# Depthwise convolutions of one layer: joined bands as the stationary operand, wide moving planes, the 1x5 taps on ScalarE and VectorE, loop written out

## The reference

```
y = _dw_conv(x, dw_w1, dw_b1, ((1, 1), (1, 1)))     # 3x3 per channel
y = _dw_conv(y, dw_w2, dw_b2, ((0, 0), (2, 2)))     # 1x5 per channel, along the row
y = _dw_conv(y, dw_w3, dw_b3, ((2, 2), (0, 0)))     # 5x1 per channel, down the column
y = conv 1x1 with pw_w over channels                 # phase C
return y * x                                         # phase C
```

## Time and profile before

| | |
|---|---|
| median of 3 runs | 4150.91 us (4149.14 to 4152.14) |
| the profiled execution | 4150.77 us, span 4149.2 us |
| PE busy, of the span | 3270.8 us, 79% |
| PEld busy (weight loads) | 2521.2 us, 61% |
| DVE, ACT, POOL busy | 73%, 66%, 34% |
| phase B | from about 2161 to 2985 us |

### The profile page before, as it was taken

The page is one execution under the profiler, slowest core; times in us unless marked ns, Lnnn a source line. Parts: engine busy times, 40 slices in busy tenths (PEclk is TensorE's granted clock), DMA queues, the critical chain, the costliest instruction groups (busy, mean ns, idle before and its releaser), DMA issues. The chain is left out here.

```text
span 4149.2 us, 80812 instructions
## 1 busy us (share of the span) xinstructions
PE 3270.8 (79%) x26660; PEld 2521.2 (61%) x26660; DVE 3025.8 (73%) x7852; ACT 2745.2 (66%) x6274; POOL 1425.2 (34%) x1892
## 2 busy tenths in 40 slices
PE   6767677776777767777659999999788778787777
PEld 5655555555555555555539999999744444444443
DVE  4888888888888888888852222222288988988987
ACT  2577777777777777777762222222189999999998
POOL 3555655556555565555420000000022222222221
PEclk8788888888888888888769999999889999999999
DMA  3133232332323323232235566566576666666662
GB/s 64 45 77 81 73 77 62 77 80 74 78 62 77 80 75 77 62 78 64 60 102 160 159 165 167 159 165 167 155 199 183 178 177 184 180 180 182 180 180 79
DMA packets 733898, 490.45 MB, mean 118 GB/s; under 512 B 420797, under 2 KB 712957, under 8 KB 721277
## 3 DMA queue, kind: packets, MB, share of 16 engines
q1 hardware_dynamic: 733564, 486.32, 44.5%
HBM read 284.42 MB, written 201.33 MB: 117 GB/s over the span
## 5 line engine op out<-in xcount | busy, mean ns | idle before, releaser
L1794 POOL TENSOR_SCALAR C_var<-C_st 128x16 f32<-128x16 f32 x64 | 16.3, 254 | 1697.4 <-DVE C_st L178 1697.4
L1331 PE MATMUL B_ps_row<-B_g,B_z 128*128 128x128 f32 x4608 | 555.8, 277 | 0.6 <-ACT B_g L1363 0.6
L1331 PEld LDWEIGHTS B_ps_row<-B_g,B_z 128*128 128x128 f32 x4608 | 532.1, 193 | 0.7 <-ACT B_g L1363 0.7
L361 ACT ACTIVATE A_h<-A_hid 128x512 f16<-128x512 f32 x768 | 426.5, 591 | 66.7 <-PE A_hid L348 63.1
L1424 DVE TENSOR_TENSOR B_mid<-B_ps_row,B_row_bias 128x512 f32<-128x512 f32 x192 | 132.8, 691 | 458.3 <-PE B_ps_row L1331 448.3
L166 POOL TENSOR_TENSOR A_rstd<-A_var,A_expo 128x16 f32<-128x16 f32 x128 | 454.2, 3549 | 23.7 <-POOL A_var L163 23.6
L178 DVE BATCH_NORM_STATS2 A_st<-A_xT 128x6 f32<-128x192 f32 x1536 | 443.6, 349 | 24.8 <-ACT A_xT L826 11.5
L361 ACT ACTIVATE C_h<-C_hid 128x512 f16<-128x512 f32 x768 | 426.1, 592 | 15.0 <-PE C_hid L348 7.7
L1461 ACT ACTIVATE C_q<-C_xT,C_shift,C_rstd 128x96 fp8e5<-128x96 f32 x1024 | 391.4, 456 | 40.9 <-POOL C_shift L1801 40.9
L369 DVE TENSOR_SCALAR A_hq<-A_h,A_b 128x512 f16<-128x512 f16 x768 | 250.0, 363 | 198.3 <-ACT A_h L361 193.3
L856 ACT ACTIVATE A_xc<-A_xT,A_shift,A_rstd 128x96 f32<-128x96 f32 x1024 | 379.0, 456 | 0.0
(11 more groups left out here) (162 smaller groups left out, 7509.5 us busy)
## 6 DMA issues: line engine op xcount, KB each, us to landing
A_xq<-in_x SPq DMA_DIRECT2D x32, 1536.0 KB, 8.9
x_scratch<-A_xT SPq DMA_DIRECT2D x64, 768.0 KB, 3.2
x_scratch<-A_x3h SPq DMA_DIRECT2D x64, 768.0 KB, 5.4
B_z<-x_scratch SPq DMA_DIRECT2D x96, 512.0 KB, 5.0
y_scratch<-B_y SPq DMA_DIRECT2D x96, 512.0 KB, 3.7
C_x3q<-x_scratch SPq DMA_DIRECT2D x32, 1536.0 KB, 9.2
C_y3q<-y_scratch SPq DMA_DIRECT2D x32, 1536.0 KB, 15.7
C_xT<-x_scratch SPq DMA_DIRECT2D x64, 768.0 KB, 15.9
```

Of the source, the lines that this page charges most:

```text
L361: act.activation(self.h16[:, k % 2, j * CH:(j + 1) * CH], self.hid2[n % 2][:], ACT.Copy).then_inc(ev["h16"], 1)
L1331: m = pe.matmul(ps_row[h][:, b * P:(b + 1) * P], z[c.buf(NB)][:, h * HB + b, d:d + W], g[c.buf(2)][:, d, :], start=(d == 0), stop=(d == 2))
```

## The change

Only phase B differs, with the host's layout of the taps.

- The taps come from the host already in the order that `flip` made, as four bands instead of five. `flip` and its tiles go, and PE waits for the loads directly.
- `joined` (was `bands`) makes the three products in one of two PSUM banks and the column sums of the last band (one column). The matmul that gave row biases goes, since a bias now stands per partition. ACT makes `g`, `row_bias` and `col_bias`, all three.
- `along_rows` takes `g` as stationary operand and four images as moving operand: 3 matmuls of 512 columns for each half, instead of 12 of 128 columns. The image isn't transposed. Four PSUM banks, two for each channel.
- ACT adds the first bias into `mid`, which now has two zeros at either side (`middle`), and writes the first of the five taps along the row into `y3` (`first_tap`: scale and bias per partition).
- DVE adds the other four taps, for each half one `scalar_tensor_tensor` (y = mid shifted * coefficient + y) of 128x512, so eight in a channel.
- `along_cols` goes.
- All buffers of a channel are released by the last of these sums: SP loads channel c+3 and stores channel c-1 after it. `y3` has three buffers.
- The 96 channels are written out, without a loop.

```diff
-        ev = Events(nc, ctx, "B_", dict(flip=1, g=1, gs=2, colb=1, rows=2, rowsb=2, cols=2, y3=2))
+        ev = Events(nc, ctx, "B_", dict(g=1, gs=3, rows=2, mid=2, first=2, sums=2 * (TAPS2 - 1)))
...
-                    sp.wait_ge(ev["cols"], ev.at("cols", c - NB, 1))
-                    sp.sem_inc(ev.passed, 1)
+                    sp.wait_ge(ev["sums"], ev.at("sums", c - NB, 2 * (TAPS2 - 1) - 1))
                 sp.dma_start(z[b][:, :, 1:W + 1], x3_dram[c.n].rearrange("b h w -> h b w")).then_inc(load_sem[b], 16)
                 t = taps[c.n]
-                sp.dma_start(band_r[b][:], bass.AP(t.tensor, t.offset, [[1, P], [TAPW, NTAP], [1, P]])).then_inc(load_sem[b], 16)
+                sp.dma_start(band[b][:], bass.AP(t.tensor, t.offset, [[1, P], [TAPW, 4], [1, P]])).then_inc(load_sem[b], 16)
                 d = dwb[c.n]
-                sp.dma_start(bias[b][:], bass.AP(d.tensor, d.offset, [[0, P], [1, 3]])).then_inc(load_sem[b], 16)
+                sp.dma_start(coef[b][:], bass.AP(d.tensor, d.offset, [[0, P], [1, 3 + TAPS2]])).then_inc(load_sem[b], 16)
...
-                sp.wait_ge(ev["y3"], ev.at("y3", c, 1))
+                sp.wait_ge(ev["sums"], ev.at("sums", c, 2 * (TAPS2 - 1) - 1))
...
+            def joined(c):
+                bd, b = band[c.buf(NB)], ps_g[c.buf(2)]
+                pe.wait_ge(load_sem[c.buf(NB)], (c.round(NB) + 1) * 48)
+                if begun(c - 2):
+                    pe.wait_ge(ev["gs"], ev.at("gs", c - 2, 2))
                 for d in range(3):
-                    pe.matmul(ps_g[:, d * P:(d + 1) * P], bd[:, d, :], bd[:, 3, :], start=True, stop=True)
-                pe.matmul(ps_s[:, 0:P], ones[:], bd[:, 3, :], start=True, stop=True)
-                pe.matmul(ps_c[:, 0:1], bd[:, 3, :], ones[:, 0:1], start=True, stop=True).then_inc(ev["g"], 1)
+                    pe.matmul(b[:, d * P:(d + 1) * P], bd[:, d, :], bd[:, 3, :], start=True, stop=True)
+                pe.matmul(b[:, 3 * P:3 * P + 1], bd[:, 3, :], ones[:], start=True, stop=True).then_inc(ev["g"], 1)
...
-                for b in range(HB):
-                    for d in range(3):
-                        m = pe.matmul(ps_row[h][:, b * P:(b + 1) * P], z[c.buf(NB)][:, h * HB + b, d:d + W],
-                                      g[c.buf(2)][:, d, :], start=(d == 0), stop=(d == 2))
+                if begun(c - 2):
+                    pe.wait_ge(ev["mid"], ev.at("mid", c - 2, h))
+                for d in range(3):
+                    m = pe.matmul(bank(c, h), g[c.buf(2)][:, d, :], z[c.buf(NB)][:, half(h), d:d + W],
+                                  start=(d == 0), stop=(d == 2))
                 m.then_inc(ev["rows"], 1)
-            def along_cols(c, h):
...
-                along_rows(c, 0)
-                if (c + 1).real:
-                    bands(c + 1)
+                if (c + 1).real:
+                    joined(c + 1)
+                along_rows(c, 0)
                 along_rows(c, 1)
-                along_cols(c, 0)
-                along_cols(c, 1)
...
+                act.activation(g[p][:], ps_g[p][:, 0:3 * P].rearrange("p (d n) -> p d n", d=3), ACT.Copy).then_inc(ev["gs"], 1)
+                act.activation(row_bias[p][:], s, ACT.Copy, scale=k[:, 0:1]).then_inc(ev["gs"], 1)
+                act.activation(col_bias[p][:], s, ACT.Identity, scale=k[:, 1:2], bias=k[:, 2:3]).then_inc(ev["gs"], 1)
...
+            def middle(c, h):
+                act.wait_ge(ev["rows"], ev.at("rows", c, h))
...
+                    act.wait_ge(ev["sums"], ev.at("sums", c - 2, 2 * (TAPS2 - 2) + h))
+                act.activation(mid[c.buf(2)][:, half(h), PAD:PAD + W], bank(c, h), ACT.Identity,
+                               bias=row_bias[c.buf(2)][:]).then_inc(ev["mid"], 1)
+            def first_tap(c, h):
+                act.wait_ge(ev["mid"], ev.at("mid", c, h))
...
+                act.activation(y3[c.buf(3)][:, half(h), :], mid[c.buf(2)][:, half(h), 0:W], ACT.Identity,
+                               scale=coef[c.buf(NB)][:, 3:4], bias=col_bias[c.buf(2)][:]).then_inc(ev["first"], 1)
...
+            def tap(c, t, h):
+                if t == 1:
+                    dve.wait_ge(ev["first"], ev.at("first", c, h))
+                else:
+                    dve.wait_ge(ev["sums"], ev.at("sums", c, 2 * (t - 2) + h))
+                y = y3[c.buf(3)][:, half(h), :]
+                dve.scalar_tensor_tensor(y, mid[c.buf(2)][:, half(h), t:t + W], coef[c.buf(NB)][:, 3 + t:4 + t], y,
+                                         ALU.mult, ALU.add).then_inc(ev["sums"], 1)
```

More of the change, by code:

```diff
@@ L40 @@
 ROUND8 = 1.5 * 2.0 ** 31
-NTAP = 5
+TAPS2 = 5
 TAPW = 2 * P - 1
@@ L1250, in phase_b @@
         NB = 4
-        ev = Events(nc, ctx, "B_", dict(flip=1, g=1, gs=2, colb=1, rows=2, rowsb=2, cols=2, y3=2))
+        PAD = TAPS2 // 2
+        ev = Events(nc, ctx, "B_", dict(g=1, gs=3, rows=2, mid=2, first=2, sums=2 * (TAPS2 - 1)))
         setup = ctx.enter_context(nc.semaphore("B_setup"))
         load_sem = [ctx.enter_context(nc.semaphore(f"B_loaded{p}")) for p in range(NB)]
-        store_sem = [ctx.enter_context(nc.semaphore(f"B_stored{p}")) for p in range(2)]
+        store_sem = [ctx.enter_context(nc.semaphore(f"B_stored{p}")) for p in range(3)]
@@ L1255, in phase_b @@
         z = [sb(f"z{p}", [P, B, W + 2], F32) for p in range(NB)]
-        band_r = [sb(f"band_r{p}", [P, NTAP, P], F32) for p in range(NB)]
-        bias = [sb(f"bias{p}", [P, 3], F32) for p in range(NB)]
-        band = [sb(f"band{p}", [P, NTAP, P], F32) for p in range(2)]
+        band = [sb(f"band{p}", [P, 4, P], F32) for p in range(NB)]
+        coef = [sb(f"coef{p}", [P, 3 + TAPS2], F32) for p in range(NB)]
         g = [sb(f"g{p}", [P, 3, P], F32) for p in range(2)]
-        row_bias = [sb(f"row_bias{p}", [P, P], F32) for p in range(2)]
+        row_bias = [sb(f"row_bias{p}", [P, 1], F32) for p in range(2)]
@@ L1261, in phase_b @@
         col_bias = [sb(f"col_bias{p}", [P, 1], F32) for p in range(2)]
[L1262 to L1268, removed]
@@ L1270, in channels, with half @@
-        def channels(eng, body):
-            sweep(eng, 0, NB, (C - 2 * NB) // NB, NB, C - 1, C - 1, body)
+        mid = [sb(f"mid{p}", [P, B, W + 2 * PAD], F32) for p in range(2)]
+        y3 = [sb(f"y3{p}", [P, B, W], F32) for p in range(3)]
+        ones = sb("ones", [P, 1], F32)
+        ps_g = [ps(f"ps_g{p}", [P, 512]) for p in range(2)]
+        ps_row = [ps(f"ps_row{p}", [P, HB * P]) for p in range(4)]
+        N_SETUP = 2 * NB + 5
+        def half(h):
+            return slice(h * HB, (h + 1) * HB)
@@ L1273, in phase_b, with bank, channels @@
+        def bank(c, h):
+            return ps_row[2 * c.buf(2) + h][:, :].rearrange("p (b n) -> p b n", b=HB)
+        def channels(body):
+            for n in range(C):
+                body(Unit(0, n, 1, C - 1))
         block = ctx.enter_context(nc.Block())
@@ L1291, in body @@
                     load(c + 3)
-                sp.wait_ge(ev["y3"], ev.at("y3", c, 1))
-                sp.sem_inc(ev.passed, 1)
-                sp.dma_start(y3_dram[c.n].rearrange("b h w -> h b w"), y3[c.buf(2)][:]).then_inc(store_sem[c.buf(2)], 16)
-            sp.wait_ge(setup, 2 * NB + 1)
+                sp.wait_ge(ev["sums"], ev.at("sums", c, 2 * (TAPS2 - 1) - 1))
+                sp.dma_start(y3_dram[c.n].rearrange("b h w -> h b w"), y3[c.buf(3)][:]).then_inc(store_sem[c.buf(3)], 16)
+            sp.wait_ge(setup, N_SETUP)
             for n in range(3):
[L1298 to L1301, removed]
+                load(Unit(0, n, 1, C - 1))
+            channels(body)
+            for p in range(3):
+                sp.wait_ge(store_sem[p], 16 * C // 3)
         @block.tensor
         def _(pe):
[L1305 to L1314, removed]
+            pe.wait_ge(setup, N_SETUP)
+            def joined(c):
[3 more added lines that the diff above has]
+                    pe.wait_ge(ev["gs"], ev.at("gs", c - 2, 2))
                 for d in range(3):
-                    pe.matmul(ps_g[:, d * P:(d + 1) * P], bd[:, d, :], bd[:, 3, :], start=True, stop=True)
-                pe.matmul(ps_s[:, 0:P], ones[:], bd[:, 3, :], start=True, stop=True)
-                pe.matmul(ps_c[:, 0:1], bd[:, 3, :], ones[:, 0:1], start=True, stop=True).then_inc(ev["g"], 1)
+                    pe.matmul(b[:, d * P:(d + 1) * P], bd[:, d, :], bd[:, 3, :], start=True, stop=True)
+                pe.matmul(b[:, 3 * P:3 * P + 1], bd[:, 3, :], ones[:], start=True, stop=True).then_inc(ev["g"], 1)
             def along_rows(c, h):
@@ L1333, in along_rows @@
-                m.then_inc(ev["rows"], 1)
-            def along_cols(c, h):
[L1337 to L1344, removed]
+                if begun(c - 2):
+                    pe.wait_ge(ev["mid"], ev.at("mid", c - 2, h))
@@ L1352, in body, with joined @@
-                along_cols(c, 1)
-            bands(first)
-            channels(pe, body)
+            joined(Unit(0, 0, 1, C - 1))
+            channels(body)
         @block.scalar
```

(49 more changed lines are left out.)

5 lines of the change are left out of this document (2 added, 3 removed).

## The result

| | before | after |
|---|---|---|
| median | 4150.89 us | 3998.66 us (3997.3 to 4003.06, 4 runs) |
| span of the profiled execution | 4149.2 us | 3997.2 us |
| ratio, 95% interval | | 0.9635 [0.9619, 0.9652] |

The kernel got 152 us faster, where 187 were forecast (3964 us, range 3900 to 4090). Phase B lasts from 2160.1 to 2833.2 us, 673 us where it was 823. Phase A ends and phase C lasts as before, within 2 us.

A forecast was written before the change was run, and what follows sets the result against it. PE alone was taken to bound phase B before the change, the loop of loads after it. 96 x (8.41 - 6.43) = 190 us less, 3.5 more at start and end: 4150.8 - 186.5 = 3964 us, range 3900 to 4090.

The forecast's parts named there:

- PE's own work: Phase B, PE: wide row passes 5.16 us plus joined bands 0.90, so 6.06 us a channel against 8.41.
- The loop of loads: Phase B: a chain of 19.3 us from load release to reuse spans three channels, so 6.43 us a channel.
- PE's body: First link of the chain: PE's own work on a channel, 6.06 us.
- End of rows to store issue: Second link of the chain: `middle`, `first_tap`, eight sums on DVE and SP's issue, 6.74 us.
- Store, loads and landing: Third link of the chain: store, image, bands and coefficients issued in turn until the last has landed, 6.5 us.
- The waits: Phase B, ahead of `joined`: PE waits about 0.4 us in each channel for its loads, released by the transfer of `coef`.
- The clock: PE in phase B: its waits cost no clock, counted as nothing; 0.9 or more expected.
- Rival 4: PE's clock falls to the lower level: 12 us of PE a channel, about 4500 us; chance 0.03.
- 1 (PE stays the bound): Phase B: loads return within 5.4 us or sums are shorter, 6.06 us a channel, 3928 us; chance 0.70 together with the forecast.
- 2 (loads later): Phase B transfers go out in a burst and meet the store: 4125 us, or 4045 at half the delay; chance 0.13.
- 3 (two cycles an element): DVE's eight sums take 1.13 us each, 9.04 us a channel: slower, 4218 us; chance 0.11.
- 5: PE's wide pass is cheaper than in phase C: PE at 3.5 us, 5.6 us a channel, 3884 us; chance 0.03.

The follow-up runs named there:

- nb6: The changed kernel with six buffers for the loads instead of four, loads going out five channels ahead: 3926.95 us, ratio 0.9463.
- nb3: The changed kernel with three buffers for the loads instead of four: 4404.39 us, ratio 1.0614.
- early_release: The changed kernel with image and band buffers released by PE's last row matmul instead of the last sum, six buffers for coefficients only: 3929.78 us, ratio 0.9466.
- imm_scalar: The changed kernel with a constant 0.5 in place of the coefficient per partition in the eight sums: 3980.1 us.
- load_first: The changed kernel with a channel's three loads issued ahead of the store that the same sum releases, instead of behind it: 3945.32 us, ratio 0.9503.

## Why the prediction was right, and where its sizes were off

**PE's own work.** 6.06 us were predicted, and 6.04 measured in nb6, where nothing else is in the way. The mechanism is right; that the sum fits this well is partly luck. The price of a float32 pass of 512 columns, read from phase C, held at 128 rows, but the break between the halves makes twelve take 5.23 us, not 5.16; and the bands with their single columns take 0.81, not 0.90. Narrow planes turned out at 5.44 / 48 = 0.113 us a pass, so the width saved 0.21 us a channel, a bit less than my 0.29. The figure of the Trainium skill, "TensorE: Matmul & The Clock Gate" (Back-to-back issue gap), 216 ns at 512 columns, is half of the 0.43 us that these float32 passes are apart.

**The loop of loads.** Right in kind, and shown from three sides: more buffers (nb6), fewer (nb3), an earlier release (early_release). Its links, as medians over the changed kernel's channels, against the 19.3 us that I summed:
- PE's body: 6.06 predicted, about 6.1 measured.
- End of rows to store issue: 6.74 predicted, 7.08 measured. To `middle` 0.20, `middle` 0.59, `first_tap` with its hand-over 0.84, as priced. The eight sums take 5.43, not 4.89: they come every 0.67 us, not 0.60, mostly because of the scalar per partition (imm_scalar). I had priced them by tensor_tensor alone. SP issues 0.03 us behind them instead of my 0.22, which made up a part.
- Store, loads and landing: 6.5 predicted, 6.9 measured, 2.4 from the store's issue to that of the coefficients and 4.4 until PE starts. I had taken the register work and a fifth of the bands off the issues. The row of the bands' issue (1.21, then mostly 1.34 to 1.37 us) didn't shrink. With the store moved behind the loads it is 0.58, though the image still goes ahead (load_first): what held it is the store's data in front.

This gives 20.1 us, 6.70 a channel. The measured mean is 6.82.

**The waits.** PE waits as forecast for the transfer of `coef`, but not 0.4 us in each channel: the loop gathers it in one wait of 1 to 2 us in about every third. On the average of the phase, `joined` starts 0.63 us later behind the last row pass than in nb6. The idle time that the trace shows, 30.6 us in 400 or 0.52 a channel, is less, since a row pass is drawn until 0.24 us after the next could start.

**The clock.** I counted it at nothing, from phase C's 0.99 at 80% busy. That was nearly right: 8.5 us were lost in the five low stretches above, 0.09 us a channel. Phase C was still an uncertain neighbour, since here some waits of about 2 us do bring the lower level. Rival 4 had the mechanism but as all or nothing, a clock low throughout; it came as a small part. In nb3, with waits of over 7 us, it is a large one: the body from 2413.67 to 2422.79 takes 9.12 us instead of 6.04.

**The sum.** 6.43 + 0.01 + 0.11 + 0.14 + 0.13 = 6.82: PE's body, end of rows to store issue, the load leg, and a rest of which 0.09 is the clock. 0.39 x 96 = 37 us, and the miss is 35. So two thirds of it lie in two links of the chain that were priced too low.

**The rivals.** 1 (PE stays the bound) is what nb6 and early_release show, at 3927 and 3930 us where it said 3928. 2 (loads later) has a piece of truth: the store ahead does delay them, by 1.7 us, but that was in my landing times and issues already. 3 (two cycles an element) is refuted by 747 ns. Here the trace and the Trainium skill, "Vector Engine (DVE) Microarchitecture Reference" (Points that are easy to get wrong), differ: the halving that it states for two SBUF sources that aren't bf16 doesn't show in these sums, and the measurement decides. 5 is refuted by nb6.

**Where the gain went.** Removing the column and bias matmuls takes 18 x 0.1136 = 2.05 us of PE in a channel, 197 us, and the width 19 to 20; the rest is in the bands and their single columns. Six buffers keep all of it (222 us). The change as made gave 72 us back: 0.78 us in each of 91 channels, of which 63 us in all are waits ahead of `joined` and the slower start behind them (0.91 us to the first row pass instead of 0.81), and 8.5 the clock.

**Not settled.** The issue of the image load holds SP for about 1.5 us or more now and then (eight times in the phase, 2.28 us at 2415.15, where 0.58 is usual), 9.5 us over the usual in all. A load stands in the chain once in three channels, so that makes some 0.04 us of the 6.82 on the average. Why it happens wasn't tried.

## What to carry to other kernels

When the engine that bounds a stage gets faster, and its result now passes through two more engines before the buffers are released, add up the chain of work and transfers from one channel to the reuse of its buffer, and divide it by the number of channels that it spans (here the buffers less one, since `joined` runs one channel ahead of the rows); that quotient is the pace if it is above the engine's own time. Put the transfers that somebody waits for ahead of those that nobody waits for in one queue, and price them by the data ahead of them. A loop gathers its idle time in one place, and a wait of 2 us on TensorE cost here, in five cases, 1.7 us more in passes at half the clock; with the shorter waits of the same kernel nothing was added.

## What was not expected of the hardware

- A float32 pass costs by its columns, almost without a fixed part: 0.113 us for 128 with a weight load for each, 0.43 for 512. Weight loads of 128x128 float32 hid almost fully even when PEld was busy 400.00 of 400 us: four 128-column passes took 0.45 us, one of 512 took 0.43.
- The order of two transfers in one queue moved the landing of a 512 KB load from 5.3 to 4.1 us, and the hold of SP by the bands' issue behind it from 1.34 to 0.58 us.
- After a wait of 2.0 us on PE the granted clock was 0.51 for the next 2 us and 0.63 for two more. This followed five waits of 1.86 to 2.09 us, and none of 24 that were of 1.2 to 1.87 us.
